# A fused Mamba-2 block with two mixture layers: projections of x issued seven units ahead, a new weight order and group tail, and B·C copies on ScalarE

## The reference, cut to what matters

```python
proj = hidden_states @ in_proj_w.T
gate, xBC, dt = jnp.split(proj, [INTER, INTER + CONV_DIM], axis=-1)
xBC = silu(causal_conv4(xBC) + conv_b)          # 4 taps over tokens
x, Bm, Cm = jnp.split(xBC, [INTER, INTER + NG * SS], axis=-1)
y  = ssd(x, Bm, Cm, D, dt)                      # decay-masked (C B^T) applied to x*dt, plus x*D
yg = y * silu(gate)
rstd = rsqrt(mean(yg**2 over the group's 1024 channels) + EPS)
out = (yg * rstd) * norm_w @ out_proj_w.T
```

## Time and profile before

| | |
|---|---|
| median of 3 runs | 1625.21 us (1624.32 to 1627.58) |
| the profiled execution's own time | 1627.01 us |
| its span, first to last instruction | 1625.2 us |
| TensorE matmul busy | 1564.3 us (96%) |
| VectorE / ScalarE / GpSimd busy | 1228.0 / 1002.3 / 1052.0 us |
| mean granted TensorE clock | 0.989 |

### The profile page before, as it was taken

One profiled execution on the slowest core, in us unless ns is written; L12 is line 12 of the kernel. 1 busy time (PEld: TensorE's weight loads), 2 busy tenths in 40 slices (PEclk: granted clock), 3 DMA queues, 4 the chain that ended last, 5 costly groups with the idle time before them and its releaser, 6 DMA issues. The chain is left out here.

```text
span 1625.2 us, 25474 instructions
## 1 busy us (share of the span) xinstructions
PE 1564.3 (96%) x8296; PEld 1226.0 (75%) x8296; DVE 1228.0 (76%) x1689; ACT 1002.3 (62%) x2122; POOL 1052.0 (65%) x790
## 2 busy tenths in 40 slices
PE   6979999999999999999999999999999999999979
PEld 4657777777777777777777777777777777777757
DVE  6688877787778877887688877887688877887565
ACT  4357765666666665666666665666666665666431
POOL 2017874788757874788657874787657874787620
PEclk9899999999999999999999999999999999999989
DMA  3033321323222221222212321223222221322011
GB/s 118 1 103 103 107 91 59 92 91 92 78 72 92 92 92 59 91 92 92 78 72 92 92 91 59 92 92 92 78 75 88 92 92 59 98 86 84 20 40 53
DMA packets 73658, 131.65 MB, mean 81 GB/s; under 512 B 10944, under 2 KB 10944, under 8 KB 73280
## 3 DMA queue, kind: packets, MB, share of 16 engines
q1 hardware_dynamic: 73536, 130.09, 24.3%
HBM read 127.44 MB, written 2.62 MB: 80 GB/s over the span
## 5 line engine op out<-in xcount | busy, mean ns | idle before, releaser
L892 DVE SCALAR_TENSOR_TENSOR mx_acc<-bank,mx_cw,mx_acc 128x510 f32<-128x510 f32 (+2 forms) x480 | 358.3, 746 | 160.8 <-ACT mx_acc L877 149.5
L159 PE MATMUL bank<-h_hi,mx_w_hi 128*128 128x512 f32 x1152 | 465.6, 404 | 4.4 <-DVE mx_acc L892 2.3
L161 PE MATMUL bank<-h_hi,mx_w_lo 128*128 128x512 f32 x1152 | 453.1, 393 | 0.0
L160 PE MATMUL bank<-h_lo,mx_w_hi 128*128 128x512 f32 x1152 | 450.2, 391 | 0.0
L1108 ACT ACTIVATE mx_mix<-mx_csb,mx_gncs 128x256 f32<-128x256 f32 x512 | 218.9, 499 | 284.3 <-PE bank L1478 281.3
L1033 POOL TENSOR_TENSOR mx_y<-mx_y,mx_sg 128x512 f32<-128x512 f32 x128 | 338.4, 2644 | 59.7 <-DVE mx_y L1280 51.7
L839 POOL TENSOR_TENSOR mx_w_lo<-mx_w_raw,mx_w_hi 128x512 fp32r<-128x512 f32 x144 | 187.4, 1302 | 111.0 <-ACT mx_w_hi L834 111.0
L161 PEld LDWEIGHTS bank<-h_hi,mx_w_lo 128*128 128x128 f32 x1152 | 216.9, 188 | 48.5
L159 PEld LDWEIGHTS bank<-h_hi,mx_w_hi 128*128 128x128 f32 x1152 | 217.3, 189 | 47.8 <-issue 6.5
L160 PEld LDWEIGHTS bank<-h_lo,mx_w_hi 128*128 128x128 f32 x1152 | 217.7, 189 | 41.5
L1262 DVE TENSOR_TENSOR mx_mix<-mx_mix,mx_cbt 128x1536 f32<-128x1536 f32 x128 | 224.5, 1754 | 0.0
(11 more groups left out here) (163 smaller groups left out, 2203.7 us busy)
## 6 DMA issues: line engine op xcount, KB each, us to landing
mx_csb<-cs_rows SPq DMA_DIRECT2D x128, 512.0 KB, 4.0
mx_w_raw<-in_w_in SPq DMA_DIRECT2D x144, 256.0 KB, 4.0
mx_wo_raw<-in_w_out SPq DMA_DIRECT2D x64, 256.0 KB, 4.2
res<-in_x SPq DMA_DIRECT2D x8, 256.0 KB, 5.0
f_base_raw<-in_base_wt SPq DMA_DIRECT2D x2, 1024.0 KB, 6.1
out<-res SPq DMA_DIRECT2D x8, 256.0 KB, 2.0
f_a_raw<-in_lora_a SPq DMA_DIRECT2D x2, 256.0 KB, 3.8
f_lb_raw<-in_lora_b SPq DMA_DIRECT2D x2, 256.0 KB, 6.2
```

Source lines behind the costliest of these rows:

```text
L159: nc.tensor.matmul(out, w_hi, x_hi, start=first, stop=False)
L160: nc.tensor.matmul(out, w_hi, x_lo, start=False, stop=False)
L161: return nc.tensor.matmul(out, w_lo, x_hi, start=False, stop=last)
L892: self.nc.vector.scalar_tensor_tensor(dst, src[:, :, 0:SEQ - k], self.cw[:, c, TAPS - 1 - k:TAPS - k], dst, ALU.mult, ALU.add).then_inc(s[ ...
```

## The change

`LEAD = 7`: in step st TensorE projects unit st+7, in every step (steps 13 to 15 take units 0 to 2 of the next group; the last group has none left there). Unit order among B and C becomes B half 0, B half 1, C half 0, C half 1. The tail keeps four projections instead of five, and the start, before step 0 of group 0, has PRJ(0) to PRJ(6) instead of PRJ(0) to PRJ(5). Weight tiles are loaded, rounded and split in the new order `ORDER`, still one per step. `keep_bc` moves from VectorE to ScalarE. `square` moves behind `tanh_conv` on ScalarE. The copy `gncs` of the decay constants goes; the activations read `m.ncs`. SyncE's loop over groups is unrolled. The wait of `transpose_x` on `ms` stays as it is.

```diff
+LEAD = 7
 def unit_of(u):
     if u < 4:
-        return u % 2, u // 2, u % 2
+        return u // 2, u % 2, u // 2
+def ahead(g, st):
+    u = st + LEAD
+    return (g, u) if u < UNITS else (g + 1, u - UNITS)
+def first_needed(g, st):
+    if st % 2 == 1:
+        return (g, 3 + st + 1) if st < STEPS - 1 else (g + 1, 2)
+    j = st // 2 + 2
+    return (g, 2 + 2 * j) if j < XT else (g + 1, (j - XT))
+def weight_order():
+    order = [(0, 0), (0, 1), (0, 2), (0, 4), (0, 3)]
+    for g in range(NG):
+        order += [first_needed(g, st) for st in range(STEPS)] + [(g + 1, 4), (g + 1, 3)]
 ...
 # InProj.evacuate
         elif u < 8:
-            act.wait_ge(s["cb"], 1 + 2 * g + (u - 4) // 2 + 1)
+            act.wait_ge(s["cb"], 1 + 2 * g + u % 2 + 1)
 ...
 # ScalarE, a step
+                    ip.round_w(act, 5 + WPG * g + st)
                     if st > XT:
                         keep_first_quad(g, st - 1)
-                        evacuate(gn, un)
-                    if st >= 1:
-                        square(g, st - 1)
+                    if gu < NG:
+                        evacuate(gu, un)
 ...
+                        tanh_conv(gu, un)
+                    if st >= 1:
+                        square(g, st - 1)
 # ScalarE, the tail
+                    evacuate(g + 1, 3)
+                    ip.round_w(act, 5 + WPG * g + STEPS)
                     square(g, STEPS - 1)
+                    tanh_conv(g + 1, 3)
+                    keep_bc(g + 1, 0)
                     evacuate(g + 1, 4)
+                    ip.round_w(act, 5 + WPG * g + STEPS + 1)
                     tanh_conv(g + 1, 4)
+                    keep_bc(g + 1, 1)
+                    evacuate(g + 1, 5)
+                    tanh_conv(g + 1, 5)
                     root(g)
+                    evacuate(g + 1, 6)
+                    tanh_conv(g + 1, 6)
 # VectorE, the tail
                     head_constants(g + 1)
-                    taps(g + 1, 1)
 ...
                     taps(g + 1, 3)
                     silu_conv(g + 1, 3)
                     taps(g + 1, 4)
                     silu_conv(g + 1, 4)
+                    taps(g + 1, 5)
+                    silu_conv(g + 1, 5)
+                    mean_square(g)
+                    taps(g + 1, 6)
+                    silu_conv(g + 1, 6)
 # TensorE, start, step and tail
             ip.project(pe, 0, 3)
             b_dot_c(0, 0)
             ip.project(pe, 0, 4)
+            b_dot_c(0, 1)
             ip.project(pe, 0, 5)
-            b_dot_c(0, 1)
+            ip.project(pe, 0, 6)
 ...
-                    if 0 < st < STEPS - 1:
-                        ip.project(pe, g, st + 5)
+                    gu, un = ahead(g, st)
+                    if gu < NG:
+                        ip.project(pe, gu, un)
 ...
                     ip.project(pe, g + 1, 3)
                     b_dot_c(g + 1, 0)
+                    ip.project(pe, g + 1, 4)
+                    sum_over_channels(g, 0)
+                    b_dot_c(g + 1, 1)
+                    ip.project(pe, g + 1, 5)
                     sum_over_channels(g, 1)
-                    ip.project(pe, g + 1, 4)
-                    ip.project(pe, g + 1, 5)
-                    b_dot_c(g + 1, 1)
+                    ip.project(pe, g + 1, 6)
```

More of the change, by code:

```diff
@@ L814, in __init__, with load_w @@
         self.acc = sb("acc", [P, 4, HB, SEQ])
[L816 to L819, removed]
+    def load_w(self, sp, n):
+        if n >= len(ORDER):
+            return
+        if n >= 3:
+            sp.wait_ge(self.s["wlo"], 1 + n - 2)
+        g, k = ORDER[n]
+        sp.dma_start(self.w_raw[:, n % 3, :, :], self.w_in[g, k, :, :, :]).then_inc(self.raw_in[n % 3], 16)
     def load_constants(self, sp, g):
@@ L1007, in group @@
                     load_late(g + 1)
-            loop_groups(sp, group)
+                    ip.load_w(sp, 5 + WPG * g + STEPS + 1)
+                    ip.load_w(sp, 5 + WPG * g + STEPS + 2)
+            for g in range(NG):
+                group(g, g + 1 < NG)
         @block.gpsimd
@@ L1148, in keep_first_quad, with keep_bc @@
                 nc.scalar.activation(m.gacc[:, n, :], O_BANK[p % 2][:, :], ACT.Copy).then_inc(s["gcopy"], 1)
+            def keep_bc(g, hf):
+                act.wait_ge(s["cb"], 1 + 2 * g + hf + 1)
+                act.wait_ge(s["mix"], 1 + STEPS * g)
+                banks = Y_BANK if hf == 0 else O_BANK
+                for b in range(HB):
+                    last = nc.scalar.activation(cbt[:, hf, b, :], banks[b][:, 0:PAIR], ACT.Copy)
+                last.then_inc(s["cbt"], 1)
             def root(g):
@@ L1161, in _ @@
             decay_from_second(0, 0)
-            ip.round_w(act, 0, 3)
+            ip.round_w(act, 3)
             tanh_conv(0, 3)
+            ip.round_w(act, 4)
+            keep_bc(0, 0)
             evacuate(0, 4)
             tanh_conv(0, 4)
+            keep_bc(0, 1)
+            for u in (5, 6):
+                evacuate(0, u)
+                tanh_conv(0, u)
             def steps(g, more):
@@ L1336, in _ @@
             silu_conv(0, 1)
[L1337 to L1344, removed]
+            for u in (2, 3):
+                taps(0, u)
+                silu_conv(0, u)
+            for u in (4, 5, 6):
+                taps(0, u)
+                silu_conv(0, u)
             def steps(g, more):
                 for st in range(STEPS):
+                    gu, un = ahead(g, st)
                     if st >= 1:
@@ L1351, in steps @@
                     scale_x(g, st)
[L1353 to L1356, removed]
+                    if gu < NG:
+                        ip.taps(dve, gu, un)
                     silu_gate(g, st)
-                    if here or more:
-                        silu_conv(gn, un)
+                    if gu < NG:
+                        silu_conv(gu, un)
                     if st % 2 == 1:
```

179 lines of the change are left out of this document (68 added, 111 removed).

## The result

| | before | after |
|---|---|---|
| median | 1625.14 us (20 runs, 1622.13 to 1629.75) | 1630.80 us (20 runs, 1625.52 to 1634.09) |
| ratio | 1 | 1.0028, 95% interval 1.0018 to 1.0039 |
| profiled execution | 1627.01, span 1625.2 | 1633.39, span 1631.6 |

The forecast was 1622.7, no change by our bound of 0.2%, with 1616.5 to 1627.5 as the range for 8 in 10. The measured median is 5.7 us above before and outside that range.

What follows compares the result with a forecast made beforehand. TensorE, 96% busy, was taken as the bound: 2.7 us gained in seven tails, less 0.2 for group 0 and end, takes 1627.0 to 1624.5, median 1622.7; own range 1620.5 to 1625, 8 in 10 from 1616.5 to 1627.5.

Steps and rivals of the forecast that it cites:

- step 1 of group 0 begins at 129.6: Start of group 0: step 1 begins at 129.6 against 121.94, with two more projections (5.7), a loss of 2.0.
- the last group gives back 5.4: End: steps 13 and 14 of the last group have no projection and take 7.57 instead of 10.28.
- the tail's wait changes its name to `mean_square`: Tail: transposes wait 1.26 us for `mean_square`, where they waited 1.88 for `silu_conv`; gain 0.39 per tail, 2.7 in seven.
- `evacuate(5)` stands 0.20 behind PRJ(5): Tail, ScalarE: `evacuate(5)` follows PRJ(5) by 0.20, the two `keep_bc` copies ahead of it costing nothing.
- the table loads have no drain: Tail, ScalarE: `root`'s two table loads cost 1.28 each, hide behind waits, and leave `mix_tokens(0)` 1.3 us of cover.
- a new wait of 0.29: Tail: `b_dot_c(1)` waits 0.29 us for `silu_conv` of unit 3, taken as 1.11 us long.
- the ring: Group 0: loop through `square`, `sum_squares`, mask, decay, weight rounding, `evacuate`, taps, tanh; 8.5 us a turn, from step 3.
- the contended ring: Steps 1 to 7 of group 0 with GpSimd and VectorE in each other's way: 56.1 us, a gain of 1.3.
- my 52.4 for a group 0 without it: Steps 1 to 7 of group 0 at 7.5 us each, before counting any hold by the loop through GpSimd.
- -0.9 for group 0 and end: Sum of start -2.0, steps 1 to 7 +1.3, end -0.2; best case +2.4, taken as -0.2.
- ScalarE's queue: Slower rival, tail: `keep_bc` copies over 0.97 for two delay `evacuate(5)`; at 1.45, 6.7 in all, 1629.4; chance 0.08.
- The rival of a tail without a wait: Tail: `mean_square` comes before PRJ(6) ends, wait wholly gone, 7 x 2.04 = 14.3, less 0.2: 1611.1; chance 0.08.

Runs made afterwards that it cites:

- Experiment 3: Kernel after with the first mask of a step issued ahead of `sum_squares` on GpSimd, `square` still late; 1619.1 us, one run.
- experiments 4: Kernel after with unit 4 projected ahead of the first `b_dot_c` at the start, unit 5 ahead of the second; 1624.9 us, one run.
- experiment 7: Kernel after with only the copies of `b_dot_c` (`keep_bc`) moved back from ScalarE to VectorE; 1631.0 us, one run.
- 8: Kernel after with the second sums and `mean_square` ahead of unit 5, and `root` ahead of `evacuate(5)`; 1624.8 us, one run.
- experiment 2: Kernel after with `square` put back ahead of `round_tile` on ScalarE; 1623.3 us, ratio 0.9998 to before.
- Experiment 5: Kernel after with first mask before `sum_squares`, second sums and `mean_square` before unit 5, `root` before `evacuate(5)`, unit 4 before first `b_dot_c`; 1614.9 us, ratio 0.9930.
- the four edits: Combined on the kernel after: first mask earlier, second sums and `mean_square` earlier, `root` earlier, unit 4 earlier at the start; together ratio 0.9930.
- 1: Kernel after with the second sum over channels ahead of PRJ(5) and `mean_square` ahead of `taps(5)` in the tail; 1625.3 us, ratio 1.0002.
- 6: Kernel after with the last `sum_squares` of a group moved behind the last weight remainder on GpSimd; 1623.1 us, one run.

## Why the prediction was wrong

- **Right**: that step 1 of group 0 begins at 129.6 (129.89; with 1.6 us of spread between traces of the same start, the closeness is partly luck), that full steps stay at 10.28, that the last group gives back 5.4, that the tail's wait changes its name to `mean_square` (1.26 forecast, 1.07 measured), that `evacuate(5)` stands 0.20 behind PRJ(5), and that the table loads have no drain: they took 1.28 each, with `mix_tokens(0)` not late.
- **The step that failed, in the tail**: "`silu_conv` at 6.96 for 1.11 us, beside GpSimd, which works in both cases ... a new wait of 0.29". It took 1.81, the wait was 0.93, and the tail 28.13 for 27.51. The tail is 0.62 above forecast, and seven times that is 4.3 us, two thirds of the 6.7 between forecast and measured at the last `mix_tokens`. Experiment 3, with `silu_conv(3)` at 1.17, has 0.29 and 27.47, so the rest of the chain was sized rightly. The mistake: a duration taken from another place of the queue, where other work of GpSimd met it at another phase. "GpSimd, which works in both cases" was true, but in the kernel before the instruction of GpSimd beside it had started earlier and ended at 633.55:

```profile
632.25 1.30 POOL L1038 TENSOR_TENSOR mx_yt_lo<-mx_y,mx_yt_hi 128x512 fp32r<-128x512 f32 x1
```

Only 0.55 of it was left when `silu_conv` started at 633.00, and 0.55 and some 0.56 of its own make the 1.11. At the new place all 1.27 were left.

- **The second term, the clock behind the ring's wait**: "with the contended ring (9.1 on average ...) it is 56.1", measured 57.51, 1.4 more. The 56.1 holds TensorE for 3.7 (56.1 - 52.4) and puts nothing for the clock; the waits were 3.0, and the 3.4 us at a granted clock of 0.52 behind them cost about 1.6. Where the clock stayed at 1.00 (experiments 4, 7 and 8) the same stretch took 55.95 to 55.98, on the forecast. The prediction charged 1.7 us for step 0 of group 0 behind an idle of over 2 us, and nothing for the wait that it gave the ring itself; it had the rows for both. The mechanism of the ring stood, and my 52.4 for a group 0 without it is what experiments 2 and 3 measured (52.6).
- **Luck in the ring's size**: the turns were 9.96, 8.87 and 9.94, 9.6 on average for my 9.1, since the mask beside `make_mix` takes 2.17 and not the 1.087 of the earlier trace rows (in the kernel before never more than 1.105, in another phase of the queues). Yet TensorE was held for less than I gave, so the slack ahead of `mix_tokens` must have been taken too small; no run separates the two.
- **The choice**: the terms gave -0.9 for group 0 and end, and I took -0.2, from a hope that lags hide behind each other; 0.7 us. The remaining 0.3 is the start. Those are the 6.7: 4.3, 1.4, 0.7 and 0.3.
- **The rivals**: none had the mechanism. ScalarE's queue, the one I gave for slower, is excluded by experiment 7. GpSimd in VectorE's way was in my text, priced for the ring only. The rival of a tail without a wait was priced too high: its 2.04 a tail is what the old wait cost, but the new sum without `mean_square` is 15.97 + 10.28 = 26.25, 1.65 less than 27.90. Experiment 5, the nearest to it, has 26.65.
- **The last part**, 2.2 us in the profiled executions, is clock: between the twelve traces it took 88.0 at a granted clock of 0.96 (experiment 2) to 93.6 at 0.87 (experiment 5), with the same instructions. Whether the change makes the low level there more frequent was not settled. The single runs of after follow the clock as well: spans of 1623.7 to 1624.3 at a mean clock of 0.990 and 0.991, of 1626.0 to 1627.7 at 0.988 and 0.989, of 1628.7 to 1632.3 at 0.983 to 0.986.

## What to carry to other kernels

When work moves on one engine, lay the timelines of VectorE and GpSimd over each other at the new place: a duration read elsewhere holds only beside the same neighbour. A lead taken on one engine shortens its own waits only if the engines behind it keep their order short; look for the ring that the move closes, and cut it where it is cheapest (here one instruction earlier on GpSimd or on ScalarE, 4.9 us). A wait that changes its name is worth following to its next name (here `silu_conv`, `mean_square`, `scale_x`, and the bank of PRJ(7)): each of the four edits gave 0.4 to 0.7 us a tail or 1 to 5 us in group 0, and they nearly added.

## What the hardware showed that I had not expected

- VectorE's `silu_conv`, with two operands in SBUF, waits out what is left of the GpSimd instruction beside it: 1.81, 1.17, 1.11 and 0.69 us with 1.27, 0.64, 0.55 and 0 of it left at its start. The other way round, the mask that starts 0.54 behind `make_mix` (162.46 to 164.67) takes 2.17 and ends 0.50 behind it. The Trainium skill (SBUF — State Buffer, "SBUF: two separate sides") states this as an exclusive lock on the port pair that both engines share: whichever starts first holds it for its whole instruction, and the other is blocked. By that rule the tail's `silu_conv(3)` would take 1.27 + 0.69 = 1.96 beside the sum, an estimate; the trace shows 1.81. I had not applied it.
- A wait of 2.74 us on TensorE can cost more than its length. In step 6 of group 0 the two waits are 3.0 us together, but steps 1 to 7 take 4.9 more than in experiment 2. The window behind the second wait shows the granted clock, near the lower level (1.2 of 2.4 GHz), and a group of four matmuls at its start takes 1.12 for 0.65:

```profile
176.90:180.30 3.40, 3.40 (x20) 2.31 (x21) 3.12 (x5) 2.67 (x8) 1.71 (x2) 0.52 0.31 77
```

Behind the same wait of 2.72 to 2.74 the clock fell in the traces of after, 1 and 6 and stayed at 1.00 in those of 4, 7 and 8. What decides between the two is not shown.
